# A fused attention and feed-forward kernel: two of five probability chunks turned by VectorE and SyncE transfers instead of TensorE, with every engine's queue reordered

## What is computed

```python
q = einsum('bsd,ed->bse', x, Wq)      # 32 query heads of 128
k = einsum('bsd,ed->bse', x, Wk)      # 8 key heads
v = einsum('bsd,ed->bse', x, Wv)
q = _rope(_rmsnorm(q, q_norm_w), pos); k = _rope(_rmsnorm(k, k_norm_w), pos)
k_all = concatenate([k_cache[block_table], k], axis=1)     # 512 cached + 128 new keys
v_all = concatenate([v_cache[block_table], v], axis=1)
scores = where(valid, einsum('bqhd,bkhd->bhqk', q, k_all) * SCALE, -1e30)
o = einsum('bhqk,bkhd->bqhd', softmax(scores), v_all)
x = x + einsum('bse,de->bsd', o, Wo)
```

## Time and profile before

| | before |
|---|---|
| median of 3 runs | 1351.88 us |
| span of the profiled execution, first to last instruction | 1349.8 us |
| TensorE busy | 1342.4 us, 99% |
| VectorE busy | 1040.8 us, 77% |
| ScalarE busy | 843.2 us, 62% |
| GpSimd busy | 713.6 us, 53% |
| granted TensorE clock | 1.00 |
| moved by DMA | 168.11 MB, mean 125 GB/s |

### The profile page before, as it was taken

The page is one execution under the profiler, slowest core; times in us unless marked ns, Lnnn a source line. Parts: engine busy times, 40 slices in busy tenths (PEclk is TensorE's granted clock), DMA queues, the critical chain, the costliest instruction groups (busy, mean ns, idle before and its releaser), DMA issues.

```text
span 1349.8 us, 24930 instructions
## 1 busy us (share of the span) xinstructions
PE 1342.4 (99%) x7812; PEld 1191.3 (88%) x7812; DVE 1040.8 (77%) x2131; ACT 843.2 (62%) x2217; POOL 713.6 (53%) x972
## 2 busy tenths in 40 slices
PE   9999999999999999999999999999999999999999
PEld 8888888888889998889888989888888888888887
DVE  7988777877787778777877787778778887748546
ACT  7676566666566556666666666566665785545444
POOL 7767465646554655565555555555555652305111
PEclk9999999999999999999999999999999999999999
DMA  5566325522552264126413641364222164354532
GB/s 201 172 185 198 87 82 173 145 63 78 187 127 59 78 201 134 38 84 206 130 31 108 203 109 31 113 210 128 79 48 48 63 191 140 125 183 141 187 141 78
DMA packets 170746, 168.11 MB, mean 125 GB/s; under 512 B 129856, under 2 KB 137664, under 8 KB 159936
## 3 DMA queue, kind: packets, MB, share of 16 engines
q1 hardware_dynamic: 164928, 131.21, 33.3%
q0 software_dynamic: 5760, 36.18, 8.1%
HBM read 133.81 MB, written 33.55 MB: 124 GB/s over the span
## 4 chain that ended last, share of the span: by engine, by line
PE 98%; POOL 1%; DVE 1%; ACT 1%; issue 0%; POOLq 0%; DVEq 0%
PE ps L64 27%; PE ps L63 27%; PE ps L65 27%; PE ps L1131 10%; PE ps L1109 2%; PE ps L1153 1%; PE ps L2038 1%; PE ps L1103 1%; PE ps L2071 0%; PE ps L2070 0%; PE ps L2024 0%; PE ps L2023 0%; PE ps L1332 0%; DVE at_scores L897 0%; PE ps L2009 0%; ACT at_mask L601 0%
## 5 line engine op out<-in xcount | busy, mean ns | idle before, releaser
L502 POOL TENSOR_SCALAR at_probs<-at_probs,at_row_inv 128x640 f32<-128x640 f32 x256 | 211.8, 828 | 151.1 <-DVE at_row_inv L903 150.9
L605 ACT ACTIVATE at_pT_hi<-ps 128x512 fp32r<-128x512 f32 x320 | 186.5, 604 | 101.1 <-PE ps L65 50.9
L897 DVE CUSTOM_DVE_ANT_0 at_scores<-ps,at_mask,at_inv_rms 128x640 f32<-128x640 f32 x256 | 220.2, 879 | 31.7 <-PE ps L65 30.8
L653 ACT ACTIVATE at_probs<-at_scores,at_neg_max 128x640 f32<-128x640 f32 x256 | 211.9, 836 | 51.0 <-DVE at_neg_max L897 51.0
L845 DVE TENSOR_TENSOR at_pT_lo<-ps,at_pT_hi 128x512 fp32r<-128x512 f32 x320 | 212.6, 686 | 25.7 <-ACT at_pT_hi L605 20.7
L63 PE MATMUL ps<-ds_hi,x_hi 128*128 128x512 f32 (+1 forms) x564 | 192.7, 342 | 0.0
L65 PE MATMUL ps<-ds_hi,x_lo 128*128 128x512 f32 (+1 forms) x564 | 192.0, 340 | 0.0
L648 ACT ACTIVATE at_square<-ps 128x128 bf16<-128x128 f32 x256 | 67.1, 276 | 166.7 <-DVE a_raw L876 149.9
L1131 PE MATMUL ps<-ident,at_probs 128*128 128x128 f32 x1280 | 160.6, 273 | 0.0
L63 PE MATMUL ps<-at_kT_hi,ds_lo 128*128 128x320 f32 x512 | 158.1, 309 | 1.6 <-DVE at_neg_max L897 1.6
L65 PE MATMUL ps<-at_kT_hi,ds_lo 128*128 128x320 f32 x512 | 158.2, 309 | 0.0
(11 more groups left out here) (215 smaller groups left out, 3379.6 us busy)
## 6 DMA issues: line engine op xcount, KB each, us to landing
kT_pages<-shared SPq DMA_DIRECT2D x16, 1024.0 KB
kv_raw<-kT_pages SPq DMA_DIRECT2D x60, 256.0 KB, 4.0
v_pages<-shared SPq DMA_DIRECT2D x14, 1024.0 KB
kv_raw<-v_pages SPq DMA_DIRECT2D x56, 256.0 KB, 4.1
sw_wgu_raw<-in_sw_gu SPq DMA_DIRECT2D x22, 512.0 KB, 3.3
staging<-in_L_cond_Wo SPq DMA_DIRECT2D x8, 1024.0 KB, 4.8
staging<-in_L_cond_Wq SPq DMA_DIRECT2D x7, 1024.0 KB
sw_b_raw<-in_sw_bgu SPq DMA_DIRECT2D x88, 64.0 KB, 2.8
```

Source lines behind the costliest of these rows:

```text
L502: pool.tensor_scalar(probs[:, h, :], probs[:, h, :], row_inv[:, h:h + 1], 1.0, ALU.mult, ALU.mult).then_inc(probs_done, 1)
L605: act.activation(out, src, ACT.Copy).then_inc(done, 1)
L653: act.activation(probs[:, h, :], scores[h % 2][:], ACT.Exp, bias=neg_max[:, h:h + 1], scale=-1.0, accum_out=row_sum[:, h:h + 1]).then_inc( ...
L897: dve.tensor_tensor_reduce(out=scores[h % 2][:], in0=slot(h), in1=mask[:, b, :], scale=inv_rms[b % 2][:, h:h + 1], scalar=3.0e38, op0=ALU. ...
```

## The change

For 62 of the 64 rounds, all but the very first and the very last (`by_moves`), chunks 3 and 4 of the probabilities (`MOVED = 2`) no longer go through TensorE. VectorE transposes the 32x32 squares of these 256 columns, one instruction per head (`turn_squares`), into a new tile `turned`. It does this at the end of the round before. SyncE then copies quarter `a` of the partitions, square column `k`, to partitions `32k` to `32k+31` of a second new tile, `pT_raw`: 4 by 4 transfers of 32 rows with 1 KB each (`move_turned`). ScalarE and VectorE make the high and low parts from `pT_raw` in SBUF instead of from a PSUM bank.

All five queues are in a new order. On TensorE `output` of a sequence stands in the next round, behind that round's transposes; `queries` stands one round earlier, at the end; `times_v` 0 and 1 stand between the scores 1 and 2, and `times_v` 2, 3 and 4 behind `project_kv`. The other engines follow. GpSimd issues the page fetches at the head of its round, ahead of `key_scale`, and rotates queries ahead of keys. Four semaphores were merged into two. The scratch space for transfers issued by GpSimd is set to 8192.

```diff
+        MOVED = 2
+        turned = sb("turned", [P, NQ, MOVED, G, SQ])
+        pT_raw = sb("pT_raw", [P, NQ, MOVED, G, SQ])
...
+        def by_moves(g, b):
+            return not (isinstance(g, int) and (g, b) in ((0, 0), (HK - 1, B - 1)))
...
+            def move_turned(g, b):
+                wait_apart(sp, turned_done, upto(g, b, G), passed)
+                for a in range(NQ):
+                    for k in range(NQ):
+                        sp.dma_start(pT_raw[k * SQ:(k + 1) * SQ, a], turned[a * SQ:(a + 1) * SQ, k]).then_inc(pT_moved[b % 2], 16)
...
             def group(g, last):
                 for b in range(B):
                     g2, b2 = following(*following(g, b))
+                    if by_moves(g, b):
+                        move_turned(g, b)
...
@@ gpsimd @@
-                    if more2:
-                        key_scale(g2, b2)
+                    if first and 2 <= b < 6:
+                        stage_pages(g, b - 2)
+                    if not first and not last and 1 <= b < 5:
+                        stage_pages(g, b - 1)
...
@@ scalar @@
+                if by_moves(g, b) and c >= KC - MOVED:
+                    hi(pT_hi[c % RING][:].rearrange("p (h a r) -> p h a r", h=G, a=NQ), moved_chunk(c), pT_moved[b % 2], moved_count(g, b), pT_hi_done[c])
...
+                    if more:
+                        exps(g1, b1, 0)
+                        exps(g1, b1, 1)
                     if b == B - 3 and not last:
                         qkv_group(g + 1, 0)
                         qkv_group(g + 1, 1)
...
+                    if by_moves(g, b):
+                        for c in range(KC - MOVED, KC):
+                            probs_T(g, b, c)
                     if more:
                         exps(g1, b1, 2)
+                        exps(g1, b1, 3)
+                    if more2:
+                        squares(g2, b2)
...
@@ vector @@
+            def turn_squares(g, b, h):
+                wait_apart(dve, probs_done, upto(g, b, G, h + 1), passed)
+                dve.transpose(turned[:, :, :, h, :].rearrange("p k c r -> p c k r"),
+                              probs[:, h, (KC - MOVED) * P:KEYS].rearrange("p (c k i) -> p c k i", c=MOVED, k=NQ)).then_inc(turned_done, 1)
...
+                    if more and by_moves(g1, b1):
+                        for h in range(G):
+                            turn_squares(g1, b1, h)
...
@@ tensor @@
-                    probs_T(g, b, 0)
-                    probs_T(g, b, 1)
+                    for c in range(KC - MOVED):
+                        probs_T(g, b, c)
+                    if started:
+                        output(*preceding(g, b))
                     if more:
-                        queries(g1, b1)
                         new_keys(g1, b1)
-                    for c in range(2, KC):
-                        probs_T(g, b, c)
-                    times_v(g, b, 0)
-                    times_v(g, b, 1)
...
+                    if by_moves(g, b):
+                        times_v(g, b, 0)
+                        times_v(g, b, 1)
                     if more:
                         score(g1, b1, 2)
-                    times_v(g, b, 4)
-                    if more:
                         score(g1, b1, 3)
                     if more3:
+                        pe.wait_ge(k_turned, upto(g, b, 1, 3))
                         project_kv(*following(g2, b2))
...
+                    for c in range(2, KC):
+                        times_v(g, b, c)
+                    if more2:
+                        queries(g2, b2)
...
-    nc = bacc.Bacc("TRN2", target_bir_lowering=False, num_devices=1)
+    nc = bacc.Bacc("TRN2", target_bir_lowering=False, num_devices=1, dynamic_dma_scratch_size=8192)
```

More of the change, by code:

```diff
@@ L245, in attention @@
         pT_done = sem("pT_done")
+        turned_done = sem("turned_done")
+        pT_moved = [sem(f"pT_moved{j}") for j in range(2)]
         pv_done = sem("pv_done")
@@ L554, in group @@
                         stage_first_keys(1)
-                    if first and 2 <= b < 6:
-                        stage_pages(g, b - 2)
-                    if not first and not last and 1 <= b < 5:
-                        stage_pages(g, b - 1)
-                    if more2 and not (last and b == B - 3):
+                    if more2:
                         rotate_q(g2, b2)
+                        rotate_k(g2, b2)
                     if more:
@@ L563, in group @@
                             normalise(g1, b1, h)
-                    if last and b == B - 3:
-                        rotate_q(g2, b2)
                     if more2:
@@ L716, in group @@
                     g2, b2 = following(g1, b1)
-                    more, more2, more3 = (not (last and b >= B - n) for n in (1, 2, 3))
+                    more, more2 = (not (last and b >= B - n) for n in (1, 2))
+                    started = not (by_row(g) and b == 0)
+                    if started:
+                        attended(*preceding(g, b))
+                    if more2 and started:
+                        key_squares(g2, b2)
+                    if more:
+                        queries(g1, b1)
                     probs_T(g, b, 0)
                     probs_T(g, b, 1)
+                    if more and started:
+                        new_values(g1, b1)
+                        cached_keys(g1, b1)
+                        cached_values(g1, b1)
                     if more:
-                        queries(g1, b1)
                         new_keys(g1, b1)
@@ L792, in group @@
                         qkv_group(g + 1, 3)
+                    if last and b == B - 1:
+                        attended(g, b)
+                        sums(2)
+                        dense.x1_hi(act, 3, X1_BANK[3])
+                        for c in range(DC - 2):
+                            dense.part_hi(act, 3, c)
             group(0, False)
@@ L986, in group @@
                         dense.x1_lo(dve, 2, X1_BANK[2])
+                    if last and b in EFF_BEFORE_TURN:
+                        dense.weights(dve, *EFF_BEFORE_TURN[b])
+                    if more2:
+                        turn_q(g2, b2, 0)
+                        turn_q(g2, b2, 1)
+                    if last and b == B - 3:
+                        dense.weights(dve, 2, 0)
+                    if more:
+                        mask_and_max(g1, b1, 0)
+                        mask_and_max(g1, b1, 1)
                     if more2:
@@ L1171, in _ @@
             idle(10, Q_BANK)
+            queries(0, 1)
             def group(g, first, last):
@@ L1194, in group @@
                     if more2:
-                        project_q(g2, b2, range(DC // 2 if last and b == B - 3 else DC))
+                        project_q(g2, b2, range(DC))
                     if more:
+                        pe.wait_ge(pT_done, upto(g, b, KC, 2))
                         score(g1, b1, 0)
@@ L1219, in group @@
                         dense.x1_turn(pe, 3, X1_BANK[3])
-                    output(g, b)
-                    if last and b == B - 1:
+                        output(g, b)
                         dense.product(pe, 2)
```

231 lines of the change are left out of this document (109 added, 122 removed).

## The result

The changed kernel takes **1425.8 us** (median of 4 runs, 1422.1 to 1430.9) where the kernel before takes 1351.9: a ratio of 1.0547, 95% interval 1.0522 to 1.0572. It is slower by 74 us, and 104 us above the forecast of 1322. The profiled execution spans 1429.1.

The account below looks back on a forecast made before the run. TensorE was taken to bound the kernel. Span 1349.8 - 52.7 (transposes) + 5.0 (seams) + 10.5 + 2 + 6 (added terms) = 1320.6; runs lie 2.1 above, so 1322 us, range 1303 to 1358.

Parts of the forecast that it names:

- What bounds, and what TensorE loses: TensorE bounds the round; eight transposes fewer save 0.85 us, a seam costs 0.08: 16.60 becomes 15.83.
- The VectorE transpose: VectorE's 256-column transposes: 0.45 us shown, 0.35 to the next, adding 1.4 to its round, 14.0 of 15.83.
- Rival 2: VectorE the new bound at 0.62 a transpose, about 1344; or a port shared with GpSimd, 1335; chance 0.17.
- The issue: SyncE's 16 issues at 0.45 us each: last starts 6.8 later, bytes land 1.3 to 2.1 before due.
- rival 3: Transfers late at 0.62 us per SyncE issue: ScalarE waits, 0.9 a round lost, 1379, slower than before; chance 0.13.
- One round in eight, and the moves behind it start late: SyncE's queue where the next group's weights load: moves behind them start late; elsewhere 512 KB more are no load.
- the layout: New queues laid out over an ordinary round: nothing late, 0.4 to 0.5 us in hand, so the round is TensorE's.
- rival 4: TensorE's gain eaten exactly: seams, waits and heavy rounds give back 0.8 us a round, 1352; chance 0.05.
- Term (a): ScalarE's weight parts make the sixth round about 1 late, the next about 0.5, in seven groups: +10.5 us.
- Term (c): VectorE's low parts of moved chunks and GpSimd's normalisations hinder each other in SBUF: 0.1 a round, +6 us.
- Term (b): Groups 0 and 7: VectorE has up to 15.49 us, and 1.4 more is above 15.83: +2 us.

Follow-up runs that it names:

- experiment 13: Changed kernel with 5 transfers a round instead of 16: one writes the turned tile to DRAM, four read it back; 1379.0 us, ratio 1.0191.
- the last version: Changed kernel with five transfers over DRAM, waits moved, groups written out without the loop, only the linear layer's matrix loaded early; 1341.3 us, 0.9916.
- early loads alone: Changed kernel with the next group's weights and the linear layer's matrix loaded a round earlier; 1405.7 us, ratio 1.0392.
- all three together: Changed kernel with 5 of 16 transfers issued by ScalarE, loads a round earlier, and groups written out without the loop; 1360.7 us, ratio 1.0065.
- experiment 5: Changed kernel with issues split over two queues: the last 5 of 16 transfers issued by ScalarE instead of SyncE; 1401.3 us, ratio 1.0354.

## Why the prediction was wrong

- **What bounds, and what TensorE loses: right.** Freed of its waits, an ordinary round is 15.7 to 15.9 (15.74 from 591.14 to 606.88); the text had 15.83. Inside the loop it is 16.04 to 16.07; in experiment 13 TensorE's weight loads wait 0.27 of that for GpSimd's last normalisation (12.5 us in 47 waits). Why this shows in the loop alone stays open.
- **The VectorE transpose: right.** Taken as 0.45 shown and 0.35 to the next; measured 0.425 at the median and 0.33 to the next. The 0.62 estimated from the Trainium skill ("VectorE: DVE Perf Modes", "The three transpose paths") isn't borne out, and the measurement decides. Rival 2's VectorE bound falls with it: VectorE is busy 78%. `oT_lo` does stand right behind the last transpose (505.99 behind 505.62), but is in time for TensorE.
- **The issue: the step that failed.** "I take 0.45, between the first two since these are half as many rows." Rows don't set it (597 ns for 64, 591 for 32). It is 0.63 from one issue to the next, which is the 0.62 that the earlier trace rows had shown and the text put down to full rings. With it, rival 3's own working has the last issue start 9.3 into the round and the bytes land at 12.1; it started at about 10.0, and ScalarE had them at 11.9. The rival was right in mechanism and place, and was given 0.13. Both rows that 0.45 was taken from are loads from DRAM, and the trace of before had no direct transfer to go by; reads from DRAM held the queue 0.43 in experiment 13 too. Why a direct one holds it longer isn't shown.
- **What rival 3 left out.** It priced 56 us; the loss against the forecast was 104. In an ordinary round it said 0.9 late, and 0.7 is measured over groups 2 to 7 (16.55 against 15.83). The rest lies in single rounds. "One round in eight, and the moves behind it start late" looked the wrong way: the weights stand behind the moves, and that costs 1.5 to 3.8 us in a sixth round (18.15 to 20.38 against 16.6). The matrix costs 12 in the last group's third round, and TensorE's stop of 11.72 for the masks wasn't in it either: the layout asked what else stands in SyncE's queue for an ordinary round alone.
- **Two sums of the text.** Rival 3 "decides at 0.8 us a round lost": in its own working, 1323 + 62 x 0.47 already makes 1352, which is 0.59 per issue and not 0.61, and so still nearer to the 0.62 of the earlier trace rows. Rival 3 and half of rival 4 are 0.155, not 0.14.
- **The loop branch: not foreseen.** The order of VectorE's work was laid out within a round. What VectorE would do first in a new pass, now `oT_lo` with TensorE waiting for it, wasn't asked. 2 to 4 us in each of five passes, the half clock behind the idle time included.
- **Term (a)** was near: with the branch away, sixth and seventh rounds are 16.6 and 16.3, 1.3 us together against 1.5. **Term (c)** is there, and larger in GpSimd's time than was taken: the median of a normalisation hardly moves (806 ns for 803), but the mean goes from 828 to 892, since one in four, beside the low part of a moved chunk, takes 1.06 to 1.17 us. That is 0.26 a round for 0.1. In the changed kernel it lies on the loop above; in the last version ordinary rounds are at TensorE's own 15.8 all the same. **Term (b)** was too small. With the terms shared out, the forecast has the first group about 2 us shorter than before, groups 2 to 7 together 23, and the last group 4. In the last version they are 6.0 longer, 24 shorter and 6 longer (133.7 for 127.3 us, to its last `output`). So the 18 us that its span is still above the forecast are 8 in the first group and 10 in the last; in groups 2 to 7 first rounds of 16.9 instead of 15.8 (ScalarE's output weights) are made up for elsewhere. TensorE's stops in the first group end with VectorE's low parts; which wait holds the two groups wasn't tried further.
- **The gains don't add.** From the changed kernel, early loads alone gave 20, the split 25, the branch 4, and all three together 65, not 49: each wait taken away exposed the next, and taking away the branch alone bought next to nothing.

## What to carry to other kernels

Price small transfers by their number: lay the issues out on their queue one behind the other, at the largest step that the trace shows in a row of them, and then ask what else stands in that queue. Where two partitions' blocks must change places, a write to DRAM and a few wide reads can beat many direct transfers. When an order is changed inside a hardware loop, look at which instruction comes first after the branch on each engine, and whether another engine waits for it.

## What the runs showed of the hardware

- An SBUF-to-SBUF transfer holds SyncE 0.59 us (median) for 32 rows and 0.60 for 64, and the next starts after 0.63 or 0.64. In experiment 5 ScalarE's five took 3.1 to 3.8, beside SyncE's eleven in 6.9 (median): two queues issue side by side.
- A store of 512 KB into DRAM had landed 2.7 us after its issue, and reads of 128 KB held the queue 0.43 us each.
- A VectorE operation with two SBUF operands beside a GpSimd normalisation stretched it from 0.80 to 1.06 us (1.17 in the last version).
- Behind a branch back, VectorE's first instruction started 2.6 to 2.9 us late, five times out of five, and had no such wait when the groups were written out. The Trainium skill ("Runtime: NRT & Kernel Launch", section "Instruction fetch mechanics") says that a taken branch whose target isn't in the engine's instruction window forces a fetch before execution goes on. The trace fits that for VectorE here, and doesn't show the fetch. In the kernel before VectorE wasn't late behind its branch.
- TensorE, idle for 2.16 us, ran its next six matmuls at 0.23 us each and the following ones at 0.43, the lower of its two clocks (1.2 for 2.4 GHz). Behind 2.00 us idle, at 682.03, the same came within 1 us.
- A register load on SyncE took 0.84 us for the address and 0.46 for the value (medians of eight), and eight of them with their checks 13.8 us in a row.
